# Moving the expert-weight casts from GpSimd to ScalarE, with other PSUM banks for the attention and an earlier output store

## The chip, the cores and the metric

The kernel runs on one Trainium2 chip, on all 8 of its NeuronCores. Each core computes one batch element (2048 tokens of width 1024) and holds the whole set of weights to itself; nothing passes between the cores. The metric is the device time in microseconds (us) of the slowest core.

## What is computed

Two transformer layers, with a layer norm ahead of each. The layer's input, its attention and its feed-forward part are added up:

```python
xn = layernorm(x)
x = x + L0_attn(xn, Wq, bq, Wk, bk) + L0_moe(xn, Wr, W1, W2)
xn = layernorm(x)
x = x + L1_attn(xn, Wq, Wk, Wv, Wo) + L1_ffn(xn, weight, alpha, bias)
```

- L0_attn: 16 heads of 64, no mask; the values are the keys (v = k).
- L0_moe: 8 experts, W1 [8, 1024, 4096] and W2 [8, 4096, 1024]. All 8 experts are computed for every token, `relu(h @ W1) @ W2`, and the two with the largest router values are summed with weights.
- L1_attn: 16 query heads, 4 key/value heads, rotary embedding, causal.
- L1_ffn: one matrix of 1024 x 1024 whose entries are set to -1, 0 or 1.

## The kernel before

The activations stay in SBUF, features on the partitions: `xT` (float32) and its normed copy `xnT` (bf16), each as 8 chunks of 128 features by 2048 tokens. Tokens are worked in 4 tiles of 512 (`NTAU`, `NT`). Each engine has one queue that is filled in the order in which the Python code emits instructions; a small class `PB` adds the semaphore waits from keys that an instruction reads and writes (`pb.op(engine, ...)`, `pb.dma(queue, ...)`). No scheduler reorders anything: an instruction that waits holds up everything that was emitted behind it on its engine.

The stages, in the order of emission: layer norm 0; attention 0; the mixture of experts; layer norm 1; attention 1; the ternary feed-forward part with the output projection of attention 1 woven in; the store.

**Attention.** `attn_stream_gen` works through tiles of 512 queries for a pair of heads. For each block of 128 keys (`kc`) TensorE writes two score blocks into banks 0 and 1, or 2 and 3 for odd `kc` (L339); ScalarE takes the exponential of both in one instruction (L362); TensorE then multiplies the previous block's exponentials with the values (L352) and accumulates 65 rows for each of the two heads in a bank of its own. Here these are banks 4 and 5 (`bankB` in the profile) for even tiles, and 6 and 7 (`bank`) for odd tiles. The finish of a tile (the reciprocal of the row sums: L444, L447 on ScalarE, L450, L452 on VectorE, L454, L458 on TensorE, L462, L469, L473 on VectorE; in layer 1 L1058 to L1078) is emitted in the next tile, at its `kc == 1`, ahead of that tile's first L352. In attention 0 the projections of the next pair of heads (L495, L502, L516, L523, moved out of PSUM by ScalarE in L506, L527, L530) are woven in: one such chunk, then three steps of the stream. They use banks 2 and 3. There are 8 pairs of heads with 4 tiles each in either layer.

**Experts.** The weights come as float32. For each of the 8 experts 16 pieces of W1 (128x2048) and 32 pieces of W2 (128x1024) are loaded into one of two slots of `stg`, cast to bf16 into the single buffer `castb` (L701, L718) and stored to DRAM (`sw1`, `sw2`). The loads, the casts and the stores all stand in GpSimd's queue, in the order load, cast, store, load, and so on, 384 times; each store also waits for the store before it. GpSimd has nothing else to do, so this queue runs from the time that the slots of `stg` are free of attention 0's own weights, beside attention 0 and the expert computation. All 384 steps are emitted ahead of the expert computation. That one runs over experts and token tiles: for each group of four blocks SyncE's queue loads 1 MB of bf16 W1 into `w1buf`, TensorE does 8 matmuls for each of 32 blocks (L749) into banks 0 to 3 in turn, and ScalarE applies relu (L757) from the bank into `hid`; then 8 x 32 matmuls with W2 (L770), scaled and added by VectorE (L778, L782). Ahead of it stands the router: 16 short chains in which ScalarE has one instruction each (L665).

**Store.** The last eight instructions of GpSimd's queue store the eight chunks of `xT`, 1 MB each. `xch(dc)` is final once both of that chunk's updates (L1239, L1136) for the four token tiles are done; the loop finishes one chunk after the other.

Of the kernel before, what the change touches and what calls it, by code (L numbers as in the profile page):

```python
# [12 lines left out]
AX = mybir.AxisListType  # L13
# [137 lines left out]
def build_nc(stages=ALL_STAGES, dbg=None):  # L151
# [27 lines left out]
    out_t = out_d.rearrange("(c p) t -> c p t", p=128)  # L179

    with ExitStack() as ctx:
# [139 lines left out]
        def attn_stream_gen(tiles):  # L321
# [8 lines left out]
            for ti, t in enumerate(tiles):  # L330
                nkc = t["nkc"]
                av0 = 4 + 2 * (ti % 2)
                for kc in range(nkc + 1):
# [11 lines left out]
                    if kc >= 1:  # L345
                        kp = kc - 1
                        qp = 2 * (kp % 2)
                        for h12 in range(2):
                            q4 = qp + h12
                            avb = av0 + h12  # L350
                            pb.op("tensor",
                                  lambda e, kp=kp, h12=h12, q4=q4, avb=avb, t=t, nkc=nkc: e.matmul(  # L352
                                      bank[avb][0:65, :], t["vap"](kp, h12),
                                      t["expb"][:, q4 * NT:(q4 + 1) * NT],
                                      start=(kp == 0), stop=(kp == nkc - 1)),
                                  reads=[f"e{q4}", t["vkeys"][h12]],
                                  writes=([f"b{avb}"] if kp == nkc - 1 else []),
                                  wait=(pb._dep_waits((), [f"b{avb}"]) if kp == 0 else []))
# [20 lines left out]
                for h12 in range(2):  # L379
                    pending_fin[h12] = (lambda t=t, h12=h12, avb=av0 + h12:  # L380
                                        t["fins"][h12](avb))
# [6 lines left out]
        def emit_attn0(xn_done):  # L388
# [49 lines left out]
            def mk_fin(h12, tgt_fn):  # L438
                def fin(avb):
# [40 lines left out]
            def prologue_chunks(hp):  # L480
# [29 lines left out]
                for mt in range(16):  # L510
                    def ktm(mt=mt, hp=hp, par=par, vA=vA, vB=vB):
                        bnk = bank[2 + (mt % 2)]
                        bkkey = f"b{2 + (mt % 2)}"
# [21 lines left out]
                def norms(hp=hp, par=par, qT=qT, kT=kT):  # L535
                    for (src, skey, coli) in ((qT, f"qT{par}", 0), (kT, f"kT{par}", 4)):
                        pb.op("vector", lambda e, src=src: e.tensor_tensor(
                            expb[:, :], src[:], src[:], ALU.mult),
                            reads=[skey], writes=["e0", "e1", "e2", "e3"])
                        for tau in range(NTAU):  # L540
                            pb.op("tensor", lambda e, tau=tau: e.matmul(
                                bank[2][0:1, :], onescol[:, :],
                                expb[:, tau * NT:(tau + 1) * NT], start=True, stop=True),
                                reads=[f"e{tau}", "onescol"], writes=["b2"])
                            pb.op("vector", lambda e, tau=tau, coli=coli: e.reduce_max(
                                CP[0:1, coli + tau:coli + tau + 1], bank[2][0:1, :], AX.X),
                                reads=["b2"], writes=[f"cp{coli + tau}"])
# [17 lines left out]
                        bank[2][:, 0:1], onesf[:, :], CP[0:1, 11:12],  # L565
                        start=True, stop=True),
                        reads=["cpn", "onesf"], writes=["b2"])
                    pb.op("vector", lambda e, par=par: e.tensor_copy(
                        CP[:, 12 + par:13 + par], bank[2][:, 0:1]),
                        reads=["b2"], writes=[f"neg{par}"])  # L570
# [38 lines left out]
        def emit_moe0(xn_done):  # L609
# [80 lines left out]
            for ex in range(NEXP):  # L690
                for fg in range(8):
                    for half in range(2):
# [8 lines left out]
                        pb.op("gpsimd", lambda e, slot=slot: e.tensor_copy(  # L701
# [6 lines left out]
                for dc in range(8):  # L708
                    for qt in range(4):
# [8 lines left out]
                        pb.op("gpsimd", lambda e, slot=slot: e.tensor_copy(  # L718
# [70 lines left out]
        def emit_attn1(xn_done):  # L789
# [150 lines left out]
            for kvc in range(2):  # L940
                for tau in range(NTAU):
                    t0 = tau * NT
                    pj = 2 + tau % 2
# [10 lines left out]
                for mt in range(16):  # L954
                    bnk = bank[2 + mt % 2]
                    bkkey = f"b{2 + mt % 2}"
# [16 lines left out]
            for kvc in range(2):  # L973
# [4 lines left out]
                for tau in range(NTAU):  # L978
                    pb.op("tensor", lambda e, tau=tau: e.matmul(
                        bank[2][0:1, :], onescol[:, :],  # L980
                        expb[:, tau * NT:(tau + 1) * NT], start=True, stop=True),
                        reads=[f"e{tau}", "onescol"], writes=["b2"])
                    pb.op("vector", lambda e, tau=tau: e.reduce_max(
                        CP[0:1, tau:tau + 1], bank[2][0:1, :], AX.X),
                        reads=["b2"], writes=[f"cp{tau}"])
# [13 lines left out]
            for hp in range(DCH):  # L999
# [6 lines left out]
                for tau in range(NTAU):  # L1006
                    t0 = tau * NT
                    pj = 2 + tau % 2
# [12 lines left out]
                for tau in range(NTAU):  # L1021
                    pb.op("tensor", lambda e, tau=tau: e.matmul(
                        bank[2][0:1, :], onescol[:, :],
                        expb[:, tau * NT:(tau + 1) * NT], start=True, stop=True),
                        reads=[f"e{tau}", "onescol"], writes=["b2"])
                    pb.op("vector", lambda e, tau=tau: e.reduce_max(
                        CP[0:1, tau:tau + 1], bank[2][0:1, :], AX.X),
                        reads=["b2"], writes=[f"cp{tau}"])
# [17 lines left out]
                    bank[2][:, 0:1], onesf[:, :], CP[0:1, 11:12],  # L1046
                    start=True, stop=True),
                    reads=["cpn", "onesf"], writes=["b2"])
                pb.op("vector", lambda e: e.tensor_copy(CP[:, 13:14], bank[2][:, 0:1]),
                      reads=["b2"], writes=["neg1"])  # L1050

                def mk_fin1(h12, ytgt, ybase, t0):
                    def fin(avb):
                        bb = h12
# [227 lines left out]
        if dbg == "xn0":  # L1282
            for dc in range(DCH):
# [74 lines left out]
```

How the kernel before makes its waits and increments, by code:

```python
            def body(eng):  # L131
                for w, fn, incs in ops:
                    for s, c in w:
                        eng.wait_ge(sems[s], c)
                    ins = fn(eng)
                    for s, n in incs:
                        ins.then_inc(sems[s], n)
```

## Time and profile before

| | us |
|---|---|
| median of 2 runs (7091.28 and 7559.44) | 7325.36 |
| profiled execution | 7085.0 |
| span of its slowest core (core 1) | 7083.5 |
| spans of the 8 cores | 7025.6 to 7083.5 |
| TensorE busy / ScalarE / VectorE / GpSimd | 5404.0 / 1929.0 / 1441.1 / 1063.1 |
| mean granted TensorE clock, as a share of full speed | 0.874 to 0.878 |

The span goes from the first to the last instruction of a core. Busy times of TensorE (PE) are modelled at their ends, so a stretch is best read by the start times of its instructions. All rows below are of core 1.

### The profile page before, as it was taken

The numbers are of one execution on the slowest core, as the hardware profiler recorded it, in microseconds if no ns is written. First come the engines' busy times: TensorE is split into PE (matmuls) and PEld (weight loads), VectorE is DVE, ScalarE is ACT, GpSimd is POOL, SyncE is SP. The second block draws the span as 40 slices with busy tenths as digits, with TensorE's granted clock in tenths as the row PEclk, the third lists the DMA queues.
The fourth block names the chain that finished last, engine by engine and source line by source line (L and its number), as shares of the span: only waits on it lengthen the run. The fifth ranks groups of instructions, "written<-read, shape, count | busy, mean of one in ns | idle before, by whom it ended". The sixth has DMA issues, their size and how long they took to land.

```text
span 7083.5 us, 83359 instructions; the slowest of 8 cores (7025.6 to 7083.5 us)
## 1 busy us (share of the span) xinstructions
PE 5404.0 (76%) x23303; PEld 2151.8 (30%) x23303; DVE 1441.1 (20%) x2660; ACT 1929.0 (27%) x2813; POOL 1063.1 (15%) x1169
## 2 busy tenths in 40 slices
PE   3566666664899989999889999999999635555536
PEld 0222222211344334334334444444444111111112
DVE  5211212123010101001010101010110443333335
ACT  0354454552111111111111121211112024554530
POOL 0233333333222222222222100000000000000000
PEclk9887787776999999999999999999999656666768
DMA  2434444344777777777777543444444100000012
GB/s 65 162 109 135 125 128 136 116 145 140 240 237 227 231 235 219 232 233 218 224 231 214 187 154 143 149 149 149 149 151 158 36 12 12 4 6 4 4 48 72
DMA packets 205108, 989.73 MB, mean 140 GB/s; under 512 B 23014, under 2 KB 33518, under 8 KB 137082
## 3 DMA queue, kind: packets, MB, share of 16 engines
q1 hardware_dynamic: 92922, 573.29, 23.9%
q0 software_dynamic: 111744, 411.09, 19.5%
q8 instruction: 210, 3.44, 0.2%
q14 instruction: 232, 1.90, 0.1%
HBM read 841.69 MB, written 142.61 MB: 139 GB/s over the span
## 4 chain that ended last, share of the span: by engine, by line
PE 59%; DMA 13%; ACT 12%; DVE 10%; issue 6%; DVEq 0%; ACTq 0%; SPq 0%; POOL 0%; POOLq 0%
PE bankA L749 21%; PE bankA L770 21%; ACT exp L362 7%; DMA w1buf<-sw 5%; DMA w2buf<-sw 5%; PE bankA L339 3%; PE bankB L352 2%; PE bank L352 2%; PE bankA L495 2%; ACT rtmpB L921 1%; PE bankA L1125 1%; PE bankA L1226 1%; PE bankA L516 1%; DVE rhl L452 1%; DVE xnTs L292 1%
## 5 line engine op out<-in xcount | busy, mean ns | idle before, releaser
L770 PE MATMUL bankA<-hid,w2buf 128*128 128x512 bf16 x8192 | 1797.0, 381 | 107.6 <-DMA w2buf<-sw 78.5
L749 PE MATMUL bankA<-xnTs,w1buf 128*128 128x512 bf16 x8192 | 1808.3, 383 | 79.9 <-DMA w1buf<-sw 79.7
L757 ACT ACTIVATE hid<-bankA 128x512 bf16<-128x512 f32 x1024 | 611.5, 597 | 3160.7 <-PE bankA L749 3160.7
L770 PEld LDWEIGHTS bankA<-hid,w2buf 128*128 128x128 bf16 x8192 | 798.3, 98 | 1106.3 <-issue 171.7
L749 PEld LDWEIGHTS bankA<-xnTs,w1buf 128*128 128x128 bf16 x8192 | 801.1, 99 | 1096.4 <-issue 167.5
L362 ACT ACTIVATE exp<-bankA,colpool 128x1024 bf16<-128x1024 f32 x832 | 908.8, 1113 | 486.8 <-PE bankA L339 454.5
L778 DVE TENSOR_TENSOR mtmp<-bankA,cbs 128x512 f32<-128x512 f32 x256 | 177.0, 692 | 3414.9 <-PE bankA L770 3414.9
L718 POOL CAST castb<-stg 128x1024 bf16<-128x1024 f32 x256 | 271.0, 1059 | 1458.0 <-DMA stg<-l0w 1458.0
L701 POOL CAST castb<-stg 128x2048 bf16<-128x2048 f32 x128 | 246.2, 1924 | 1032.7 <-DMA stg<-l0w 1032.7
L110 POOL DMA_DIRECT2D stg<-l0w x384 | 332.2, 865 | 219.9 <-DVE wkbf L310 201.8
L817 POOL IOTA invfr<- 1x128 f32 x1 | 0.2, 241 | 1703.6 <-ACT c L821 1703.6
L110 POOL DMA_DIRECT2D sw<-castb x384 | 210.2, 547 | 211.1 <-POOL castb L718 140.7
L450 DVE CAST rhl<-rrow 1x512 bf16<-1x512 f32 x64 | 39.0, 609 | 963.6 <-ACT rrow L447 963.6
L110 POOL DMA_DIRECT2D outT<-xTs x8 | 4.2, 536 | 1340.5 <-DVE xTs L1136 1340.5
L782 DVE TENSOR_TENSOR xTs<-xTs,mtmp 128x512 f32<-128x512 f32 x256 | 186.2, 727 | 27.3 <-DVE mtmp L778 0.9
L352 PE MATMUL bank<-exp,vG 128*65 128x512 bf16 x384 | 144.1, 442 | 56.5 <-DVE exp L373 36.6
L454 PE MATMUL bankA<-rhl,onesb 1*128 1x512 bf16 x64 | 34.2, 535 | 182.6 <-DVE rhl L450 182.6
L373 DVE TENSOR_TENSOR exp<-exp,cmaskS 128x512 bf16<-128x512 bf16 x256 | 97.4, 422 | 303.1 <-ACT exp L362 303.1
L339 PE MATMUL bankA<-qT,kT 64*128 64x512 bf16 x640 | 154.4, 466 | 0.1
L1068 PE MATMUL bankA<-rhl,onesb 1*128 1x512 bf16 x64 | 36.7, 574 | 153.1 <-DVE rhl L1064 153.1
L352 PE MATMUL bankB<-exp,vG 128*65 128x512 bf16 x256 | 108.2, 500 | 44.4 <-DVE exp L373 35.1
L339 PE MATMUL bankA<-qT0a,kT0a 64*128 64x512 bf16 x512 | 114.3, 411 | 25.3 <-ACT vB0b L530 13.6
(232 smaller groups left out, 3395.8 us busy)
## 6 DMA issues: line engine op xcount, KB each, us to landing
w1buf<-sw SPq DMA_DIRECT2D x256, 1024.0 KB, 6.9
w2buf<-sw SPq DMA_DIRECT2D x256, 1024.0 KB, 6.8
stg<-l0w POOLq DMA_DIRECT2D x128, 1024.0 KB, 7.4
stg<-l0w POOLq DMA_DIRECT2D x256, 512.0 KB, 5.6
sw<-castb POOLq DMA_DIRECT2D x128, 512.0 KB, 3.3
sw<-castb POOLq DMA_DIRECT2D x256, 256.0 KB, 3.3
xTs<-xT SPq DMA_DIRECT2D x8, 1024.0 KB, 16.6
wtf<-l1wt SPq DMA_DIRECT2D x16, 512.0 KB
```

What stands on the lines that cost most here:

```text
L110: self.on(qeng, lambda e, o=out, i=in_: e.dma_start(o, i), wait=w, inc=[(sem, 16)])
L339: lambda e, kc=kc, h12=h12, q4=q4, t=t: e.matmul(bank[q4][:, :], t["klhsT"](kc, h12), t["qrhs"][h12], start=True, stop=True),
L352: lambda e, kp=kp, h12=h12, q4=q4, avb=avb, t=t, nkc=nkc: e.matmul(bank[avb][0:65, :], t["vap"](kp, h12), t["expb"][:, q4 * NT:(q4 + 1) * NT],
L362: lambda e, pp=pp, t=t: e.activation(t["expb"][:, pp * NT:(pp + 2) * NT], bankA[:, pp * NT:(pp + 2) * NT], AF.Exp, bias=t["negcol"]),
L495: e.matmul(bnk[:, :], wbf[:, dc * 1024 + hp * 128: dc * 1024 + (hp + 1) * 128], xnch(dc)[:, t0:t0 + NT], start=(dc == 0), stop=False),
L701: pb.op("gpsimd", lambda e, slot=slot: e.tensor_copy(castb[:, 0:2048], stg[:, slot * 2048:(slot + 1) * 2048]), reads=[f"stg{slot}"], write ...
L718: pb.op("gpsimd", lambda e, slot=slot: e.tensor_copy(castb[:, 0:1024], stg[:, slot * 2048:slot * 2048 + 1024]), reads=[f"stg{slot}"], writ ...
L749: e.matmul(bnk[:, :], w1buf[:, slot * 4096 + dc * NT + fp * 128: slot * 4096 + dc * NT + (fp + 1) * 128], xnch(dc)[:, t0:t0 + NT], start=( ...
L757: pb.op("scalar", lambda e, f=f, bnk=bnk: e.activation(hid[:, f * NT:(f + 1) * NT], bnk[:, :], AF.Relu), reads=[bkkey], writes=[f"hid{f % ...
L770: e.matmul(bnk[:, :], w2buf[:, slot * 4096 + fc * 128:slot * 4096 + (fc + 1) * 128], hid[:, fc * NT:(fc + 1) * NT], start=(fc == 0), stop= ...
L778: pb.op("vector", lambda e, bnk=bnk, mslot=mslot: e.tensor_tensor(mtmp[:, mslot * NT:(mslot + 1) * NT], bnk[:, :], cbs[:], ALU.mult), read ...
L782: pb.op("vector", lambda e, dc=dc, t0=t0, mslot=mslot: e.tensor_tensor(xch(dc)[:, t0:t0 + NT], xch(dc)[:, t0:t0 + NT], mtmp[:, mslot * NT: ...
```

## The change

Five edits. The casts of the expert weights go from GpSimd to ScalarE; their loads and stores stay in GpSimd's queue. The attention's value products always use banks 4 and 5. The projections use banks 6 and 7 in place of 2 and 3 (in `norms` bank 7, in layer 1's norms bank 4). The finish in layer 1 broadcasts through banks 6 and 7 in place of 0 and 1 (in layer 0 it keeps 0 and 1). The output stores wait for their own chunk only.

```diff
@@ attn_stream_gen
-                av0 = 4 + 2 * (ti % 2)
...
-                            avb = av0 + h12
...
-                                      bank[avb][0:65, :], t["vap"](kp, h12),
+                                      bank[4 + h12][0:65, :], t["vap"](kp, h12),
...
-                                  wait=(pb._dep_waits((), [f"b{avb}"]) if kp == 0 else []))
+                                  wait=(pb._dep_waits((), [f"b{4 + h12}"]) if kp == 0 else []))
@@ prologue_chunks, proj and ktm (the same in layer 1's projections)
-                            bnk = bank[2 + tau % 2]
-                            bkkey = f"b{2 + tau % 2}"
+                            bnk = bank[6 + tau % 2]
+                            bkkey = f"b{6 + tau % 2}"
@@ emit_moe0, pieces of W1
-                        pb.op("gpsimd", lambda e, slot=slot: e.tensor_copy(
+                        pb.op("scalar", lambda e, slot=slot: e.copy(
                             castb[:, 0:2048],
                             stg[:, slot * 2048:(slot + 1) * 2048]),
                             reads=[f"stg{slot}"], writes=["castb0"])
@@ emit_moe0, pieces of W2
-                        pb.op("gpsimd", lambda e, slot=slot: e.tensor_copy(
+                        pb.op("scalar", lambda e, slot=slot: e.copy(
                             castb[:, 0:1024],
                             stg[:, slot * 2048:slot * 2048 + 1024]),
@@ mk_fin1
-                        bb = h12
+                        avb = 4 + h12
+                        bb = 6 + h12
@@ the end
-        final_waits = [("dv", pb.cnt["dv"]), ("sc", pb.cnt["sc"]),
-                       ("pe", pb.cnt["pe"]), ("gp", pb.cnt["gp"])]
         for dc in range(DCH):
-            pb.dma("gpsimd", out_t[dc], xch(dc), "dst",
-                   reads=[f"x{dc}"], wait=final_waits)
+            pb.dma("gpsimd", out_t[dc], xch(dc), "dst", reads=[f"x{dc}"])
```

ScalarE's queue around the start of the experts, before: the last finish of attention 0, the router's sixteen instructions, then the 1024 relus.

```order
L447 ACTIVATE rrow<-rrow 1x512
L665 ACTIVATE colpool<-colpool 128x1 x16
L757 ACTIVATE hid<-bankA 128x512 x1024
L259 COPY rows_ln<-bankB 1x512
L261 COPY rows_ln<-bank 1x512
```

The same place in the changed kernel, where L699 and L716 are the casts, L755 the relu and L663 the router; the dots stand for six more pairs of the two casts.

```order
L445 ACTIVATE rrow<-rrow 1x512
L663 ACTIVATE colpool<-colpool 128x1 x16
L699 CAST castb<-stg 128x2048 x16
L716 CAST castb<-stg 128x1024 x32
...
L699 CAST castb<-stg 128x2048 x16
L716 CAST castb<-stg 128x1024 x32
L755 ACTIVATE hid<-bankA 128x512 x1024
L259 COPY rows_ln<-bankB 1x512
```

All 384 casts now stand on ScalarE behind attention 0 and the router, and ahead of the first relu.

GpSimd's queue at the start of the weight steps, before, with the semaphores that each waits for (pga, pgb: the loads; ppw: the stores; gp: GpSimd's own instructions).

```order
L110 DMA stg<-l0w1 128x4x512 [waits stga,dv]
L701 CAST castb<-stg 128x2048 [waits pga]
L110 DMA sw1<-castb 128x2048 [waits gp]
L110 DMA stg<-l0w1 128x4x512 [waits stgb,dv]
L701 CAST castb<-stg 128x2048 [waits pgb,ppw]
```

The same place in the changed kernel (sc: ScalarE's instructions).

```order
L110 DMA stg<-l0w1 128x4x512 [waits stga,dv]
L110 DMA sw1<-castb 128x2048 [waits sc]
L110 DMA stg<-l0w1 128x4x512 [waits stgb,dv]
L110 DMA sw1<-castb 128x2048 [waits ppw,sc]
L110 DMA stg<-l0w1 128x4x512 [waits pga]
```

The first load still goes out early; the first store waits for ScalarE's first cast, and the second load stands behind that store.

TensorE's queue at a change of tile in attention 0, before: the finish's four small matmuls, then the new tile's first value products.

```order
L339 MATMUL bankA<-qT0a,kT0a 128x512 x2
L454 MATMUL bankA<-rhl0,onesb 128x512
L458 MATMUL bankA<-rhl0,onesb 128x512
L454 MATMUL bankA<-rhl0,onesb 128x512
L458 MATMUL bankA<-rhl0,onesb 128x512
L352 MATMUL bank6<-exp0,vA0a 65x512
L352 MATMUL bank7<-exp0,vB0a 65x512
```

The same place in the changed kernel (L350 is the value product).

```order
L338 MATMUL bankA<-qT0a,kT0a 128x512 x2
L452 MATMUL bankA<-rhl0,onesb 128x512
L456 MATMUL bankA<-rhl0,onesb 128x512
L452 MATMUL bankA<-rhl0,onesb 128x512
L456 MATMUL bankA<-rhl0,onesb 128x512
L350 MATMUL bankB<-exp0,vA0a 65x512
L350 MATMUL bankB<-exp0,vB0a 65x512
```

The order is the same; the value products now write the banks (4 and 5, `bankB`) that the previous tile's finish still has to read.

## Rows read from the trace of the kernel before

**Rows 1.** The view by stretches; columns: stretch, length, busy us (instructions) of each engine, clock, DMA share, GB/s.
```profile
1000.00:1500.00 500.00, 318.02 (x1389) 103.75 (x1387) 105.12 (x153) 248.91 (x346) 167.63 (x178) 0.79 0.43 137
1640.00:1726.00 86.00, 11.20 (x147) 7.60 (x148) 41.86 (x209) 3.24 (x16) 26.27 (x32) 0.50 0.41 122
1800.00:4000.00 2200.00, 2031.68 (x9083) 888.86 (x9081) 217.62 (x304) 334.42 (x560) 528.36 (x578) 0.98 0.75 228
4020.00:5549.00 1529.00, 1515.25 (x6967) 680.39 (x6964) 161.42 (x235) 250.78 (x420) 0.00 (x0) 1.00 0.40 148
```

**Rows 2.** The groups by line, whole span; busy us, mean ns, idle before and releaser.
```profile
L757 ACT ACTIVATE hid<-bankA 128x512 bf16<-128x512 f32 x1024 | 611.5, 597 | 3160.7 <-PE bankA L749 3160.7
L1202 ACT ACTIVATE wsgn<-wtf 128x1024 bf16<-128x1024 f32 x8 | 8.5, 1057 | 78.9 <-DMA wtf<-l1wt 68.1 <-DVE wtb L1214 10.9
```

**Rows 3.** GpSimd's timeline beside attention 0: start us, us, what, idle before.
```profile
228.75 1.89 POOL L701 CAST castb<-stg 128x2048 bf16<-128x2048 f32 x1 [6.15 <-DMA stg<-l0w]
231.19 0.53 POOL L110 DMA_DIRECT2D sw<-castb  x1 [0.54 <-POOL castb L701]
231.72 0.77 POOL L110 DMA_DIRECT2D stg<-l0w  x1
238.45 1.89 POOL L701 CAST castb<-stg 128x2048 bf16<-128x2048 f32 x1 [5.97 <-DMA stg<-l0w]
...
901.63 1.04 POOL L718 CAST castb<-stg 128x1024 bf16<-128x1024 f32 x1 [3.92 <-DMA stg<-l0w]
...
908.67 1.04 POOL L718 CAST castb<-stg 128x1024 bf16<-128x1024 f32 x1 [3.99 <-DMA stg<-l0w]
```

**Rows 4.** GpSimd's timeline: the first cast of experts 0 to 3.
```profile
208.36 2.06 POOL L701 CAST castb<-stg 128x2048 bf16<-128x2048 f32 x1 [4.96 <-DMA stg<-l0w]
...
611.12 1.89 POOL L701 CAST castb<-stg 128x2048 bf16<-128x2048 f32 x1 [5.45 <-DMA stg<-l0w]
...
1005.73 1.89 POOL L701 CAST castb<-stg 128x2048 bf16<-128x2048 f32 x1 [5.48 <-DMA stg<-l0w]
...
1394.15 1.89 POOL L701 CAST castb<-stg 128x2048 bf16<-128x2048 f32 x1 [5.60 <-DMA stg<-l0w]
```

**Rows 5.** The timeline where the experts begin, ScalarE and TensorE.
```profile
1721.38 0.20 ACT L665 ACTIVATE colpool<-colpool 128x1 f32<-128x1 f32 x1 [4.81 <-DVE colpool L662]
1729.89 0.60 ACT L757 ACTIVATE hid<-bankA 128x512 bf16<-128x512 f32 x1 [8.31 <-PE bankA L749]
...
1725.98 5.18 PE L749 MATMUL bankA<-xnTs,w1buf 128*128 128x512 bf16 x15
```

**Rows 6.** The chain that ended last, pieces of the experts: start us, us, what.
```profile
4027.00 55.41 PE bankA L770 x256
...
5493.87 55.43 PE bankA L770 x256
...
5539.79 9.51 PE bankA L770 x44
```

**Rows 7.** The end of the span: the last VectorE instruction, the stores, the time to landing.
```profile
7057.10 0.69 DVE L1136 TENSOR_TENSOR xTs<-xTs,wtmp 128x512 f32<-128x512 f32 x1
7058.55 4.22 POOL L110 DMA_DIRECT2D outT<-xTs  x8 [1340.51 <-DVE xTs L1136]
...
DMA to landing us min/median/max: 4.4/11.7/18.6
```

**Rows 8.** The timeline at a change of tile in attention 0.
```profile
841.49 0.63 PE L352 MATMUL bank<-exp,vB0b 128*65 128x512 bf16 x1
842.03 0.69 DVE L469 TENSOR_TENSOR t1s<-bankB,rb 64x512 f32<-64x512 f32 x1
```

**Rows 9.** The groups by line within 240 to 1631 us (attention 0); idle before and releaser.
```profile
L339 PE MATMUL bankA<-qT0b,kT0b 64*128 64x512 bf16 x512 | 115.2, 423 | 18.7 <-ACT vB0a L530 10.2 <-ACT kT0a L506 4.1 <-ACT qT0a L506 4.1
L339 PE MATMUL bankA<-qT0a,kT0a 64*128 64x512 bf16 x512 | 114.3, 411 | 25.3 <-ACT vB0b L530 13.6 <-ACT qT0b L506 5.8 <-ACT kT0b L506 5.5
L516 PE MATMUL bankA<-wkbf,xnTs 128*128 128x128 bf16 x896 | 78.1, 237 | 31.7 <-ACT exp L362 31.7
```

More of the change, by code:

```diff
@@ L356, in attn_stream_gen @@
                                   reads=[f"e{q4}", t["vkeys"][h12]],
-                                  writes=([f"b{avb}"] if kp == nkc - 1 else []),
-                                  wait=(pb._dep_waits((), [f"b{avb}"]) if kp == 0 else []))
+                                  writes=([f"b{4 + h12}"] if kp == nkc - 1 else []),
+                                  wait=(pb._dep_waits((), [f"b{4 + h12}"]) if kp == 0 else []))
                     if kc < nkc:
@@ L511, in ktm @@
                     def ktm(mt=mt, hp=hp, par=par, vA=vA, vB=vB):
-                        bnk = bank[2 + (mt % 2)]
-                        bkkey = f"b{2 + (mt % 2)}"
+                        bnk = bank[6 + (mt % 2)]
+                        bkkey = f"b{6 + (mt % 2)}"
                         for dc in range(DCH):
@@ L564, in norms @@
                     pb.op("tensor", lambda e: e.matmul(
-                        bank[2][:, 0:1], onesf[:, :], CP[0:1, 11:12],
+                        bank[7][:, 0:1], onesf[:, :], CP[0:1, 11:12],
                         start=True, stop=True),
-                        reads=["cpn", "onesf"], writes=["b2"])
+                        reads=["cpn", "onesf"], writes=["b7"])
                     pb.op("vector", lambda e, par=par: e.tensor_copy(
-                        CP[:, 12 + par:13 + par], bank[2][:, 0:1]),
-                        reads=["b2"], writes=[f"neg{par}"])
+                        CP[:, 12 + par:13 + par], bank[7][:, 0:1]),
+                        reads=["b7"], writes=[f"neg{par}"])
                 ch.append(norms)
@@ L954, in emit_attn1 @@
                 for mt in range(16):
-                    bnk = bank[2 + mt % 2]
-                    bkkey = f"b{2 + mt % 2}"
+                    bnk = bank[6 + mt % 2]
+                    bkkey = f"b{6 + mt % 2}"
                     for dc in range(DCH):
@@ L979, in emit_attn1 @@
                     pb.op("tensor", lambda e, tau=tau: e.matmul(
-                        bank[2][0:1, :], onescol[:, :],
+                        bank[4][0:1, :], onescol[:, :],
                         expb[:, tau * NT:(tau + 1) * NT], start=True, stop=True),
-                        reads=[f"e{tau}", "onescol"], writes=["b2"])
+                        reads=[f"e{tau}", "onescol"], writes=["b4"])
                     pb.op("vector", lambda e, tau=tau: e.reduce_max(
-                        CP[0:1, tau:tau + 1], bank[2][0:1, :], AX.X),
-                        reads=["b2"], writes=[f"cp{tau}"])
+                        CP[0:1, tau:tau + 1], bank[4][0:1, :], AX.X),
+                        reads=["b4"], writes=[f"cp{tau}"])
                 pb.op("vector", lambda e, kvc=kvc: e.reduce_max(
@@ L1022, in emit_attn1 @@
                     pb.op("tensor", lambda e, tau=tau: e.matmul(
[L1023 removed]
+                        bank[4][0:1, :], onescol[:, :],
                         expb[:, tau * NT:(tau + 1) * NT], start=True, stop=True),
[L1025 removed]
+                        reads=[f"e{tau}", "onescol"], writes=["b4"])
                     pb.op("vector", lambda e, tau=tau: e.reduce_max(
[L1027 to L1028 removed]
+                        CP[0:1, tau:tau + 1], bank[4][0:1, :], AX.X),
+                        reads=["b4"], writes=[f"cp{tau}"])
                 pb.op("vector", lambda e: e.reduce_max(CP[0:1, 8:9], CP[0:1, 0:4], AX.X),
@@ L1045, in emit_attn1, with fin @@
                 pb.op("tensor", lambda e: e.matmul(
-                    bank[2][:, 0:1], onesf[:, :], CP[0:1, 11:12],
+                    bank[4][:, 0:1], onesf[:, :], CP[0:1, 11:12],
                     start=True, stop=True),
-                    reads=["cpn", "onesf"], writes=["b2"])
-                pb.op("vector", lambda e: e.tensor_copy(CP[:, 13:14], bank[2][:, 0:1]),
-                      reads=["b2"], writes=["neg1"])
+                    reads=["cpn", "onesf"], writes=["b4"])
+                pb.op("vector", lambda e: e.tensor_copy(CP[:, 13:14], bank[4][:, 0:1]),
+                      reads=["b4"], writes=["neg1"])
                 def mk_fin1(h12, ytgt, ybase, t0):
-                    def fin(avb):
-                        bb = h12
+                    def fin():
+                        avb = 4 + h12
+                        bb = 6 + h12
                         hi = rhl1[0:1, (2 * h12) * NT:(2 * h12 + 1) * NT]
```

19 lines of the change are left out of this document (9 added, 10 removed).

## The prediction

> **What bounds the kernel now.** I read the view by stretches first [rows 1], since the shares of the whole span mix four regimes. From 4020 to 5549 us TensorE is busy for 1515 of 1529 us at a granted clock of 1.00 (2.4 GHz): the experts are pure TensorE time there, and GpSimd does nothing. From 1800 to 4000 us TensorE is busy for 2032 of 2200 us, with DMA at 0.75 and GpSimd in 578 instructions: the weight steps run beside the experts and cost them something, but do not set the pace. From 1000 to 1500 us (attention 0) GpSimd is as active, 178 instructions, while ScalarE is busy for half of the time. So the conversion of 384 weight pieces is hidden: beside attention 0, beside the router, and beside the first half of the experts. The groups by line say what ScalarE does in the expert stage [rows 2]: it waits 3161 us for the matmuls of L749 and works 611 us. It looks like an engine with room to spare. The question is where in its queue the new work stands.
>
> The two listings of ScalarE's queue under the change answer it. In the changed kernel all 384 casts stand behind attention 0 and the router and ahead of the first of 1024 relus. ScalarE can't begin a cast before attention 0 is over, and can't give a relu before the last cast is done. TensorE has four banks for L749; after four blocks of 8 matmuls it must wait for a relu. GpSimd's listing shows the other half: the second load stands behind the first store, which waits for ScalarE's first cast, so only one piece is loaded ahead. The weight conversion ceases to be hidden anywhere and becomes a stage of its own between router and experts.
>
> **The casts: length of the new stage.** Its step is the old one, load, cast, store issue, next load, in strict turn. In the timeline of GpSimd a piece of W1 takes 9.70 us from cast to cast (228.75 to 238.45): 1.89 us of cast, 0.54 us until the store is issued, 0.53 us for that, and 6.73 us from the issue of the load to the next cast; a piece of W2 takes 7.04 us (901.63 to 908.67) [rows 3]. For a whole expert, 16 + 32 pieces, I take differences of first casts while only attention runs beside [rows 4]: 402.8, 394.6 and 388.4 us. I take the last, since the new stage runs beside idle engines; 16 x 9.70 + 32 x 7.04 = 380.5 is the low bound and 402.8 the high one. Eight experts less the last changeover (8.6 us of step, of which 1.0 is cast: 7.6): 8 x 388.4 - 7.6 = 3099.6 us; bounds 3036 and 3215.
>
> ScalarE in place of GpSimd changes a step a little. The cast itself: ScalarE writes 128x1024 from SBUF float32 to bf16 in 1057 ns (L1202), GpSimd in 1040 ns [rows 2, 3], which is nothing. The handoff: cast to store is 0.54 us within GpSimd; from VectorE to GpSimd's output store it was 0.76 us (7057.79 to 7058.55) [rows 7]. No row shows ScalarE releasing such a store. From a gap of zero (-0.54 a step, -207 us) to 0.76 with as much again for the way from the load to another engine (+0.44, +169 us), I take +0.1 us a step, between the same-engine and the cross-engine row: 384 x 0.1 = +38 us.
>
> Start: the router's last ScalarE instruction is at 1721.38 [rows 5]; the first piece has long landed, so the casts begin at 1721.7. Last cast ends at 1721.7 + 3099.6 + 38 = 4859.3. The first relu came at 1729.9 [rows 5]; it moves by 3129.4 us. TensorE by then has the first four blocks ready, three of which it had not at the old first relu: 3 x 1.73 (55.41 us for 256 matmuls [rows 6]) = 5.2 us back. **Term 1: +3124 us.**
>
> **The experts alone.** With the conversion finished ahead, no weight transfer competes with the loads of `w1buf` and `w2buf`. Before, the stage took 1725.98 to 5549.30 (5539.79 + 9.51) = 3823.3 us [rows 5, 6]. Undisturbed, thirteen rounds of one expert and one token tile took 4027.00 to 5493.87, 112.84 us each [rows 6]; 32 rounds take 3610.8. **Term 2: -212.5 us.** Zero is the bound on one side (if the clock or the loads are no better), -212.5 the other.
>
> On that clock a page speaks against me. In the stretch of 4020 to 5549 us the granted clock is 1.00 [rows 1], with all eight cores at work. The Trainium skill's page "TensorE: Matmul & The Clock Gate", section "Seeing it yourself", warns that dense matmuls on most cores of a die bring the whole die to 13/16 of the clock while they last. By that rule 3610.8 us would be an estimated 4444 us; by the row it is 3610.8. The trace does not agree with the page in this stretch, so I keep the row, and give the other case as a rival.
>
> **The output stores.** They no longer wait for the end of everything: chunk 0's store goes out seven eighths of the last stage earlier, and only the last chunk stands after the last VectorE instruction. Before, 7058.55 to 7083.5 = 24.9 us followed; now one transfer follows, 4.4 to 11.7 us by its landing times, of which the least loaded is nearest: 6 us [rows 7]. The matmuls beside don't use DMA there. **Term 3: -19 us** (-13 to -20.5).
>
> **Banks 4 and 5 for every tile.** At a change of tile the second head's first value product started at 841.49, while the finish of the other pair of banks was still to read its own in L469 until 842.03 + 0.69 = 842.72 [rows 8]. Now it waits for that read; with some 0.14 us for the release, it starts at 842.86, 1.37 us later. The first head's read was over earlier and costs nothing. Behind the waiting product TensorE has the next scores and ScalarE the next exponential, so it is on the path. It happens in 3 of 4 tiles (the last tile's finish is flushed before the next pair starts), 8 pairs, 2 layers: 48 x 1.37. **Term 4: +66 us** (0 if the wait is covered, 66 otherwise).
>
> **Banks 6 and 7 for the projections.** TensorE waited 31.7 us in L516 for an exponential to free banks 2 or 3, and 18.7 + 25.3 us in L339 for ScalarE to move a projection out of them [rows 9]: 75.7 us, all gone. ScalarE is the next to be late, with 249 of 500 us busy [rows 1] not by much; I take -60 of it. **Term 5: -60 us** (-76 to 0). The finish of layer 1 through banks 6 and 7, and GpSimd's absence as a neighbour of VectorE, I put at nothing: the scores that write bank 0 next stand behind those value products in TensorE's queue anyway.
>
> **Sum**, against the profiled execution: 7083.5 + 3124 - 212.5 - 19 + 66 - 60 = 9982, plus the 1.5 us that its time lies above the span: 9984, say **9980 us**. That execution (7085.0) stands near the faster of the two runs shown (7091), 240 us under their median of 7325; the two runs lie 468 us apart, so a median of few runs of the changed kernel may lie that much above.
>
> **Rivals.** (a) *The clock.* The dense stretch grows from 1.5 ms to 3.6 ms with no gap for DMA, and the chip grants less. For it: attention 0 shows 0.79 and the far spacing of the two runs; against it: 1.00 for 1.5 ms on end [rows 1]. At 0.79 the stage takes 3610.8 / 0.79 = 4571, +960: 10940 us. The page's 13/16 would give an estimated 10815. (b) *Slow steps.* The steps take what they took beside the experts: 578 GpSimd instructions in 2200 us against 178 in 500 [rows 1] is a rate lower by 1.355, so 388.4 becomes 526 an expert and the total 11080. Against it: nothing else moves data in the new stage. (c) *Loads run ahead.* The two slots let the next load overlap cast and store: 16 x 6.7 + 32 x 4.9 (7.04 less 1.04, 0.54 and 0.53) = 264 an expert, 995 us less: 8985. Against it: the load stands behind the store in GpSimd's queue. (d) *Not slower.* The relus get past the casts, because ScalarE does not keep its emitted order or because the conversion still begins at 208 us; then the experts start at 1726 as before, and with terms 3 to 5 the time is 7072. It decides from the point where the stage costs less than 226 us, 0.6 us a step; a single cast of W2 takes 1.04. The listings exclude it unless the change does not do what it says.
>
> **How the numbers follow.** My forecast 0.86; (a) 0.06, (b) 0.03, (c) 0.03, (d) 0.01, and 0.01 for something else on the faster side. The forecast's own range comes from the bounds of stage length (-64, +115), handoff (-245, +131), term 2 (up to +212), and the rest; these ends don't come together, and some 9770 to 10230 holds it. To keep 8 in 10 with a spread of runs like that shown, I reach up to 10450. About 2% is what a measurement of this kernel can tell from no change; slower by over 2% are forecast, (a), (b), (c) and part of the rest: 0.98; within 2% 0.01; faster 0.01.
>
> **What would show it.** In the changed profile: GpSimd issues one load near 203 us and then nothing until about 1722; from there to about 4860 us TensorE is idle at a low clock, ScalarE shows 384 casts busy for about a sixth of the time, and waits for the loads, DMA at about 0.4; the relus start after the last cast; 32 rounds of 112.8 us follow at clock 1.00; the stores begin within the last stage, 6 us follow its last VectorE instruction. Wrong would be a first cast before 1600 us, relus between casts, an expert's pieces under 370 or over 410 us, a round over 114 us, or attention 0 changed by over 60 us.

## The result and the profile after

| | before | changed | prediction |
|---|---|---|---|
| median of all runs, us | 7093.7 (10 runs) | 10081.1 (11 runs) | 9980 |
| profiled execution, us | 7085.0 | 9868.8 | 9984 |
| ratio | 1 | 1.396 [1.391, 1.401] | 1.409 |

The change makes the kernel slower by 40%. In some executions the cores of one die ran at a lower clock; the interval of the ratio leaves these out and the median of 10081 holds them, so the terms are read from the profiled execution, and in the experiments from cores that were not held back, each against the same core of the other kernels.

The page's slices of the changed kernel, 247 us each (rows: busy tenths of an engine, the granted clock, the DMA share):

```profile
PE   3666661000000000000899999999999998355555
ACT  0555552111111111111111111111111111155551
POOL 0000000111111111111000000000000000000000
PEclk9878775555555555555999999999999998577777
DMA  2000002344343443443344434444444343000002
```

From slice 8 to slice 19 TensorE does next to nothing (33 instructions in the second row below) and its clock stands at 0.5 (1.2 GHz). GpSimd's work, which used to run beside attention 0 and the first half of the experts, lies in exactly those slices. The view by stretches says the same in microseconds:

```profile
240.00:1500.00 1260.00, 827.82 (x3720) 272.79 (x3717) 257.34 (x426) 682.49 (x924) 0.00 (x0) 0.78 0.00 1
1610.00:4700.00 3090.00, 9.35 (x33) 3.38 (x32) 0.69 (x1) 504.51 (x379) 529.66 (x759) 0.50 0.41 130
4730.00:8327.00 3597.00, 3567.69 (x16400) 1602.08 (x16398) 371.35 (x541) 608.48 (x1019) 0.00 (x0) 1.00 0.41 149
```

From 1610 to 4700 us ScalarE is busy for 505 of 3090 us and DMA for 0.41: no engine is busy for most of the stage. That looks like a chain of latencies; the run with loads ahead tests it. The groups by line name the waits (busy, mean ns, idle before and what ended it):

```profile
L747 PE MATMUL bankA<-xnTs,w1buf 128*128 128x512 bf16 x8192 | 1778.8, 380 | 3105.3 <-ACT hid L755 2712.5
L716 ACT CAST castb<-stg 128x1024 bf16<-128x1024 f32 x256 | 267.6, 1045 | 1579.4 <-DMA stg<-l0w 1579.4
L699 ACT CAST castb<-stg 128x2048 bf16<-128x2048 f32 x128 | 243.0, 1898 | 1026.9 <-DMA stg<-l0w 1026.9
```

The old L749 never waited for a relu. TensorE now waits once, for 2712.5 us, for the first relu. The other 392.8 us of its idle time end with weight loads, nearly all of it with the first one: L747 starts at 2003 us, once expert 0 is converted, fills its four banks and stops. ScalarE waits 2606 us for loads between its casts. The two ends of the stage in ScalarE's timeline, the last router instruction and first cast, the last cast and first relus:

```profile
1606.17 0.20 ACT L663 ACTIVATE colpool<-colpool 128x1 f32<-128x1 f32 x1 [4.09 <-DVE colpool L660]
1606.28 1.88 ACT L699 CAST castb<-stg 128x2048 bf16<-128x2048 f32 x1
...
4722.12 1.04 ACT L716 CAST castb<-stg 128x1024 bf16<-128x1024 f32 x1 [5.98 <-DMA stg<-l0w]
4723.19 2.07 ACT L755 ACTIVATE hid<-bankA 128x512 bf16<-128x512 f32 x4
```

GpSimd's timeline from its start, which answers to [rows 3, 4]: one load, then nothing for 1405 us.

```profile
202.44 0.91 POOL L110 DMA_DIRECT2D stg<-l0w  x1 [201.74 <-DVE wkbf L310]
1608.73 0.54 POOL L110 DMA_DIRECT2D sw<-castb  x1 [1405.39 <-ACT castb L699]
1609.33 0.77 POOL L110 DMA_DIRECT2D stg<-l0w  x1
```

The store goes out at 1608.73, 0.57 us after the cast's end at 1608.16, much the gap that GpSimd had behind its own cast (0.54 us). Later in the stage it is 0.54 us here too: a cast at 2403.00 lasts 1.90 us, and its store goes out at 2405.44. The chain of the expert stage, against [rows 6], has no DMA piece left:

```profile
4776.27 55.41 PE bankA L768 x256
...
8159.39 55.41 PE bankA L768 x256
...
8272.11 28.00 PE bankA L768 x129
```

Thirty rounds in 3383.1 us are 112.77 each. The end, against [rows 7]:

```profile
9859.00 0.69 DVE L1135 TENSOR_TENSOR xTs<-xTs,wtmp 128x512 f32<-128x512 f32 x1
9860.24 0.53 POOL L110 DMA_DIRECT2D outT<-xTs  x1 [13.28 <-DVE xTs L1135]
...
DMA to landing us min/median/max: 4.2/4.2/5.2
```

Stage by stage, from the first and last starts of each line (before on core 1, after on core 5, the slowest of each):

| stage | before | after | difference |
|---|---|---|---|
| start to the router's last ScalarE instruction | 1721.4 | 1606.2 | -115.2 |
| from there to the first relu | 8.5 | 3117.0 | +3108.5 |
| first relu to the last matmul of the experts | 3819.0 | 3603.9 | -215.1 |
| layer norm 1 and the rest up to attention 1 | 313.9 | 314.7 | +0.8 |
| attention 1, first projection to last exponential | 973.8 | 999.5 | +25.7 |
| up to and through the last feed-forward part | 220.5 | 217.7 | -2.8 |
| after the last VectorE instruction's start | 26.4 | 8.0 | -18.4 |
| sum | 7083.5 | 9867.0 | +2783.5 |

One row was not foreseen: the start up to the router is 115 us shorter, where 27 were forecast. The experiments go to that, and to the question whether the engine of the casts or their place makes the loss.

### The profile page after: what moved, and what is told of

The parts are those of the page before. It is cut to its first block, busy times and chain, and to the rows that moved or that the text cites. A ratio compares the mean times of both kernels' runs of the same rounds, so it can differ in the third digit from the quotient of the medians.

```text
span 9867.0 us, 84588 instructions; the slowest of 8 cores (9852.4 to 9867.0 us)
## 1 busy us (share of the span) xinstructions
PE 5307.5 (54%) x23303; PEld 2146.6 (22%) x23303; DVE 1402.8 (14%) x2660; ACT 2434.4 (25%) x3197; POOL 543.6 (6%) x785
## 4 chain that ended last, share of the span: by engine, by line
PE 47%; DMA 23%; ACT 13%; DVE 7%; issue 7%; POOL 2%; ACTq 0%; DVEq 0%; POOLq 0%; SPq 0%
DMA stg<-l0w 21%; PE bankA L768 18%; PE bankA L747 18%; ACT exp L360 5%; PE bankB L350 3%; ACT castb L716 3%; ACT castb L699 2%; POOL sw L110 2%; PE bankA L338 2%; PE bank L493 1%; ACT rtmpB L919 1%; PE bankA L1124 1%; PE bankA L1225 1%; DVE rb L1075 0%; DVE rb L460 0%
## 5 line engine op out<-in xcount | busy, mean ns | idle before, releaser
L747 PE MATMUL bankA<-xnTs,w1buf 128*128 128x512 bf16 x8192 | 1778.8, 380 | 3105.3 <-ACT hid L755 2712.5
L768 PE MATMUL bankA<-hid,w2buf 128*128 128x512 bf16 x8192 | 1773.4, 379 | 28.7 <-ACT hid L755 28.6
L747 PEld LDWEIGHTS bankA<-xnTs,w1buf 128*128 128x128 bf16 x8192 | 799.4, 98 | 4094.0 <-issue 3140.1
L755 ACT ACTIVATE hid<-bankA 128x512 bf16<-128x512 f32 x1024 | 611.1, 597 | 2937.7 <-PE bankA L747 2937.6
L716 ACT CAST castb<-stg 128x1024 bf16<-128x1024 f32 x256 | 267.6, 1045 | 1579.4 <-DMA stg<-l0w 1579.4
L699 ACT CAST castb<-stg 128x2048 bf16<-128x2048 f32 x128 | 243.0, 1898 | 1026.9 <-DMA stg<-l0w 1026.9
L350 PE MATMUL bankB<-exp,vG 128*65 128x512 bf16 x640 | 258.5, 467 | 132.4 <-DVE exp L371 75.4
L448 DVE CAST rhl<-rrow 1x512 bf16<-1x512 f32 x64 | 26.3, 411 | 879.9 <-ACT rrow L445 879.9
L350 PE MATMUL bankB<-exp,vA0b 128*65 128x512 bf16 x256 | 109.5, 428 | 60.2 <-ACT exp L360 53.6
L350 PE MATMUL bankB<-exp,vA0a 128*65 128x512 bf16 x256 | 109.2, 426 | 58.7 <-ACT exp L360 53.3
L452 PE MATMUL bankA<-rhl,onesb 1*128 1x512 bf16 x64 | 35.3, 551 | 177.1 <-DVE rhl L448 177.1
L350 PEld LDWEIGHTS bankB<-exp,vG 128*65 128x65 bf16 x640 | 61.3, 119 | 282.0 <-issue 281.9
L1067 PE MATMUL bank<-rhl,onesb 1*128 1x512 bf16 x64 | 35.8, 559 | 152.2 <-DVE rhl L1063 152.2
```

What stands on the lines that cost most here:

```text
L350: lambda e, kp=kp, h12=h12, q4=q4, t=t, nkc=nkc: e.matmul(bank[4 + h12][0:65, :], t["vap"](kp, h12), t["expb"][:, q4 * NT:(q4 + 1) * NT], ...
L699: pb.op("scalar", lambda e, slot=slot: e.copy(castb[:, 0:2048], stg[:, slot * 2048:(slot + 1) * 2048]), reads=[f"stg{slot}"], writes=["cas ...
L716: pb.op("scalar", lambda e, slot=slot: e.copy(castb[:, 0:1024], stg[:, slot * 2048:slot * 2048 + 1024]), reads=[f"stg{slot}"], writes=["ca ...
L747: e.matmul(bnk[:, :], w1buf[:, slot * 4096 + dc * NT + fp * 128: slot * 4096 + dc * NT + (fp + 1) * 128], xnch(dc)[:, t0:t0 + NT], start=( ...
L755: pb.op("scalar", lambda e, f=f, bnk=bnk: e.activation(hid[:, f * NT:(f + 1) * NT], bnk[:, :], AF.Relu), reads=[bkkey], writes=[f"hid{f % ...
L768: e.matmul(bnk[:, :], w2buf[:, slot * 4096 + fc * 128:slot * 4096 + (fc + 1) * 128], hid[:, fc * NT:(fc + 1) * NT], start=(fc == 0), stop= ...
```

## The experiments

**Only the casts.** The kernel before, with the two casts on ScalarE.

```diff
-                        pb.op("gpsimd", lambda e, slot=slot: e.tensor_copy(
+                        pb.op("scalar", lambda e, slot=slot: e.copy(
```

> The kernel before with only the casts moved to ScalarE. Theory that the place in the queue is the whole loss: 384 casts stand between router and first relu, the stage between them lasts 3117 us as in the changed kernel, the experts take 3604 us after it, total about 9960 us (9940 to 9980). Under theory P of the projection banks the router ends at 1705 to 1721 us; under theory G (GpSimd's absence) near 1620 to 1640 us, total about 9880.

Measured: 10052.7 us once; cores 4 to 7 spanned 9926.8 to 9939.2. ScalarE's timeline on core 5:

```profile
1691.16 0.20 ACT L665 ACTIVATE colpool<-colpool 128x1 f32<-128x1 f32 x1 [4.10 <-DVE colpool L662]
1691.27 1.88 ACT L701 CAST castb<-stg 128x2048 bf16<-128x2048 f32 x1
...
4793.63 2.07 ACT L757 ACTIVATE hid<-bankA 128x512 bf16<-128x512 f32 x4
```

The stage between router and relu lasts 3102 us, and the experts 3602 after it. The casts alone bring the whole loss. The router's end, 1691.2 on core 5, lies between the two forecasts for it: before it was at 1726.2 on this core. So up to there the absence of GpSimd's casts gives 35 us on core 5, and on cores 4, 6 and 7 it gives 23, 24 and 11.

**Only the casts' place.** The casts stay on ScalarE, 48 of them ahead of the first relu, the rest woven into the experts. One step (load, cast, store) is emitted at each of 12 places a round:

```diff
+            for _ in range(48):
+                one_step()
...
+                        if fg % 2 == 1:
+                            one_step()
...
+                        one_step()
```

> The changed kernel with the casts still on ScalarE, but only expert 0's 48 stand ahead of the first relu; the other 336 are woven into the expert computation, 12 in each round of one expert and one token tile (one after every second group of W1, one after each block of W2). If the place in the queue makes the loss: the first relu comes near 1606 + 391 = 2000 us, the expert stage takes 3604 to 4250 us (a conversion beside the experts took some 540 us an expert before, a round set of four takes 451), total 7150 to 7800 us. If ScalarE as the engine of the casts makes it (384 steps that cost the same wherever they stand): near 9870 us.

Measured: 7941.3 us, beside 7067.6 for the kernel before. The first relu came at 2004.7 us on core 6, 407 after the router's end at 1597.4; the experts took 4393 us, more than the 4250 I allowed. The same 384 casts on the same engine cost 874 us here against 2784, so 1900 us of the loss belong to the place. Of the 874, some 400 are the 48 casts that still stand ahead of the first relu. What is left shows at `castb` and at the relu:

```profile
L710 ACT CAST castb<-stg x384: 1036/1045/1900, 1597.5 to 5935.9; 128x1024 bf16<-128x1024 f32 x128, 128x2048 bf16<-128x2048 f32 x64
...
  DMA stg<-l0w: 2306.3, 292
  ACT hid L760: 632.0, 48
```

ScalarE waits 2306 us in 292 casts for their loads, and while it waits no relu passes; in turn the stores waited 632 us that are put down to a relu in front of the cast. The expert stage took 789 us more than the 3604 of the changed kernel. Of these TensorE waited 432 us for relus (22 times): a queue that waits, in small pieces. It waited another 256 us for weight loads; the remaining 100 were not taken apart.

**Loads ahead.** The changed kernel, with load n+1 emitted before cast and store of piece n.

```diff
+            steps[0][0]()
+            for n, (load, finish) in enumerate(steps):
+                if n + 1 < len(steps):
+                    steps[n + 1][0]()
+                finish()
```

> The changed kernel with each load issued ahead of the previous piece's cast and store. The stage between router and first relu lasted 3117 us. If it is a chain of latencies (load, cast, store issue in strict turn), overlapping the load with the rest leaves 6.7 us a piece of W1 and 4.9 us a piece of W2, 264 us an expert: the stage takes about 2110 to 2400 us, total 8860 to 9150 us. If the stage is bound by what the transfers can move (about 130 GB/s were seen), it stays at 3000 to 3117 us and the total near 9800 to 9870.

Measured: 8827.2 us, once, a little under the forecast; the stage lasts from 1599.3 to 3619.7 on core 6, 2020 us, 253 an expert. A piece of W2 takes 4.6 us where it took 7.2 (ScalarE's timeline, core 6):

```profile
1702.54 1.04 ACT L710 CAST castb<-stg 128x1024 bf16<-128x1024 f32 x1 [3.87 <-DMA sw<-castb]
1707.43 1.04 ACT L710 CAST castb<-stg 128x1024 bf16<-128x1024 f32 x1 [3.85 <-DMA sw<-castb]
1711.78 1.04 ACT L710 CAST castb<-stg 128x1024 bf16<-128x1024 f32 x1 [3.30 <-DMA sw<-castb]
```

The stage was a chain of latencies, not bound by what transfers can move: they moved 200 GB/s here (1610 to 3600 us) against 130. The wait ahead of a cast is no longer the load but the previous store, which still reads the single `castb`.

**Casts back on GpSimd.** The changed kernel without the cast edit; the rest of the change alone.

> The changed kernel with the casts returned to GpSimd; banks and stores stay as changed. It tells what the rest of the change is worth. In the changed kernel the router ended at 1606 us and not at 1721. Theory P: that gain comes from the projections' own banks, so the router ends near 1610 to 1625 here too; the total is 7085 less some 100 (attention 0) less 18 (stores) plus 26 (value banks in attention 1) plus 10 (a longer overlap of conversion and experts): about 7000 us, 1 to 1.5% faster than before. Theory G: the gain came from GpSimd's absence as VectorE's neighbour; then the router ends near 1690 to 1700 and the total is near 7075 us.

> The same kernel as in the run with the casts returned to GpSimd, on another chip and with more rounds, to settle its ratio to the kernel before. Its undisturbed cores spanned 6943 to 6984 us there, against 7035 to 7053 us before. By the terms measured (attention 0 -127 from the projections' banks, +29 and +27 from the value banks in the two attentions, stores -19) it should take 0.986 to 0.990 of the kernel before, about 6990 to 7010 us. The rival: the experts start 100 us earlier with fewer weights ready and give it back; then the ratio is over 0.995.

Cores 4 to 7 of the first run spanned 6943.2 to 6984.1 us, against 7031.4 to 7052.8 before. The second gave the ratio: 0.989 [0.985, 0.993], with a profiled span of 7004.5. The rest of the change is a gain of 1.1%, and the rival (the earlier start of the experts given back) does not hold. On core 5 of the first run the router ends at 1617.2, on cores 4, 6 and 7 at 1626 to 1635: some us later than theory P has it, and far from theory G's 1690.

**Only the value banks.** The kernel before with one number changed.

```diff
-                av0 = 4 + 2 * (ti % 2)
+                av0 = 4
```

> The kernel before with the value products always in banks 4 and 5, and nothing else changed. It measures the term that the prediction put at 1.37 us in each of 48 changes of tile. Expected by the prediction: attention 0 and attention 1 each longer by 33 us, total +66 us (0.9%). The rival: the wait hides behind ScalarE's exponential or VectorE's work and the total moves by less than 20 us. After the profile of the changed kernel (attention 1 longer by 26 us) I expect +50 to +66.

Measured: no ratio came out of this run, but cores 4 to 7 spanned 7092.0 to 7141.9 us against 7031.4 to 7052.8, +67 for the medians. The wait is there (who waited for whom, core 5, the two attentions apart):

```profile
PE bankB L352 <- DVE t1s L469: 28.3, 24, 1.5
...
PE bankB L352 <- DVE yT L1078: 28.0, 24, 1.2
```

Exactly 24 times in each, 1.18 us a time. The changed kernel's timeline shows one of them, against [rows 8]:

```profile
702.43 0.68 DVE L467 TENSOR_TENSOR t1s<-bankB,rb 64x512 f32<-64x512 f32 x1
...
703.26 0.61 PE L350 MATMUL bankB<-exp,vB0a 128*65 128x512 bf16 x1 [1.17 <-DVE t1s L467]
```

The five kernels side by side give attention 0 in parts. Each row is the last update of attention 0 (duration min/median/max in ns, first and last start), all on core 5: before; value banks only; casts back; casts only; the full change.

```profile
L473 DVE TENSOR_TENSOR xTs<-xTs,t1s x64: 683/689/2384, 306.2 to 1641.9; 64x512 f32<-64x512 f32 x64
L473 DVE TENSOR_TENSOR xTs<-xTs,t1s x64: 683/689/2125, 300.5 to 1661.8; 64x512 f32<-64x512 f32 x64
L471 DVE TENSOR_TENSOR xTs<-xTs,t1s x64: 683/689/1579, 298.5 to 1529.4; 64x512 f32<-64x512 f32 x64
L473 DVE TENSOR_TENSOR xTs<-xTs,t1s x64: 683/686/690, 298.4 to 1615.9; 64x512 f32<-64x512 f32 x64
L471 DVE TENSOR_TENSOR xTs<-xTs,t1s x64: 683/686/690, 302.0 to 1530.8; 64x512 f32<-64x512 f32 x64
```

From the first projection to that update, differences on cores 4, 5, 6 and 7: value banks +28, +20, +37, +55 us, mean +35; the projections' banks (casts back less value banks) -117, -132, -127, -135, mean -128; the casts' absence (casts only less before) -14, -24, -14, -3, mean -13. Each is one trace against one trace, and the kernel before spreads over 16 us on these cores, so the small two are known to some 10 us. In the rows the maximum falls from 2384 to 690 ns once GpSimd does no casts.

**Loads ahead, casts on GpSimd.** Both ideas that gained, together; then with the W2 pieces in the two halves of `castb` in turn.

> Casts on GpSimd, banks and stores as changed, and each load issued ahead of the previous piece's cast and store, so that it overlaps them. If a step is then load alone (6.7 and 4.9 us), an expert's conversion takes about 264 to 300 us beside attention 0 instead of 393, five experts are ready when the router ends and the rest costs the expert stage less: total 30 to 80 us under the run with the casts back, about 6930 to 6970 us. The rival: the extra transfers in flight only slow each other down and the loads of the experts, and the total stays within 20 us of the run with the casts back, or rises.

> The same kernel as in the run with casts on GpSimd and loads ahead. Its clock was low in that run's profile, so that its expert stage could not be read. Conversion ends near 2580 us instead of 3970. If that relieves the experts, the total is 30 to 80 us under the run with the casts back. If denser transfers beside attention 0 and the experts' start only cost elsewhere (attention 0 was 22 to 77 us longer there), the two are equal within 20 us.

> The version with casts on GpSimd and loads ahead, with the W2 pieces using the two halves of castb in turn, so that a cast no longer waits for the store just before it (that wait took 1180 us over 383 casts). If that wait sets the pace, a W2 step falls from 4.6 to about 4 us and conversion ends some 100 to 200 us earlier; the expert stage gains 0 to 20 us: total 0.980 to 0.985 of the kernel before. If the transfers set it, conversion ends where it did (2610 to 2690 us) and the total stays at 0.983.

```diff
+                c0 = 0 if i < 16 else slot * 1024
+                cb = castb[:, c0:c0 + wd]
+                keys = ["castb0", "castb1"] if i < 16 else [f"castb{slot}"]
```

The first run is inconclusive: its profile had a granted clock of 0.81 in the expert stage (2600 to 3900 us) and its four times run from 7064 to 7631. The second spans 6956.4 us on its slowest core against 7004.5 for the casts back, 48 less; by the lowest times, 6958.1 against 6984.0, it is 26 less. The forecast was 30 to 80, so the gain is at its lower end; no interval came out. Conversion ended between 2609 and 2692 us in place of 3867 to 3994, and the expert stage took 3706 to 3749 us (core 5: 3737, against 3778). Attention 0 changed by -10 to +20 us from core to core, +7 in the mean. GpSimd's casts there waited for the stores alone (core 4):

```profile
L710 POOL CAST castb<-stg x384: 1040/1042/2667, 208.3 to 2682.4; 128x1024 bf16<-128x1024 f32 x128, 128x2048 bf16<-128x2048 f32 x64
...
  DMA sw<-castb: 1180.4, 383
```

With the halves in turn the ratio to the kernel before is 0.978 [0.975, 0.981], a little better than the forecast of 0.980 to 0.985, and the lowest time 6924.4 us. In its profile, which had granted clocks of 0.81 to 0.82, conversion ends between 2337 and 2448 us, earlier than forecast, and on core 4 the casts' wait for the store falls from 1180 to 485 us: that wait did set the pace. That is the best version found; it beats both kernels.

## Why the prediction was right, and where a term was off

**The mechanism and the main term.** Right, with its numbers. The place of the casts in ScalarE's queue made the loss: the casts by themselves reproduce it, and with the same casts placed elsewhere two thirds of it are gone. From the router's last ScalarE instruction to the first relu it took 3117 us against a predicted 3138. Inside, two small errors cancel in part: an expert's 48 pieces took 391 us (388.4 forecast, 17 too low over eight), and the 0.1 us a step for the handoff to another engine, 38 us, does not exist: the gap is 0.54 to 0.57 us across engines and 0.54 within GpSimd [rows 3]. My other row, 0.76 from VectorE to the output store [rows 7], was the wrong one to lean on. That store waited for four engines; in the changed kernel the last store waits for its own chunk alone and goes out 0.55 us after VectorE's last instruction (9859.69 to 9860.24). That the four waits made the difference was not tested.

**The experts alone** (term 2): -212.5 forecast; from first relu to last matmul it is -215.1, of which I had booked 5.2 with term 1. Rounds of 112.77 against 112.84. The mean granted clock over these 3597 us was 1.00 (2.4 GHz) on core 5, and it was 1.00 on the other seven cores too. Rival (a) does not hold for this execution. It was a live one all the same: the casts-only kernel was granted 0.97 to 0.98 in this stage on cores 0 to 3, and the first run with casts on GpSimd and loads ahead 0.81 to 0.83 on all eight cores from 2600 to 3900 us. What decides between these clocks no run shows. The page "TensorE: Matmul & The Clock Gate" of the Trainium skill, section "Seeing it yourself", gives 13/16 for dense matmuls on three or more cores of a die. The changed kernel's trace does not agree with it; the 0.81 of that other run does.

**The stores** (term 3): -19 forecast, -18.4.

**The value banks** (term 4): 1.37 us in 48 places, +66 forecast. The place and the count were right; the price is 1.18 us (28.3 / 24), which makes 57 us of wait; the two attentions together grew by 67. In attention 1 the stage grew by 32 us on core 5 with the value banks alone (972.4 to 1004.1), and by 27 in the full change (999.5). So the full change's other edits, of which the finish and the projections through other banks touch attention 1, gave some 5 back; I had put the finish at nothing, and the two were not taken apart.

**The projections' banks** (term 5): this step failed in size, and beyond its bounds. "75.7 us, all gone. [...] I take -60 of it. Term 5: -60 us (-76 to 0)"; measured is -128 in attention 0 alone. It also set off one of my own signs of being wrong, attention 0 changed by over 60 us: it became 101 to 112 us shorter on cores 4 to 7. The sum of TensorE's waits at two lines was taken as the most that could be won. What the starts of successive key projections show is the length of the cycle instead, one chunk and three steps of the stream. Before:

```profile
711.12 0.61 PE L516 MATMUL bankA<-wkbf,xnTs 128*128 128x128 bf16 x8 [0.78 <-ACT exp L362]
715.26 0.61 PE L516 MATMUL bankA<-wkbf,xnTs 128*128 128x128 bf16 x8
720.75 0.61 PE L516 MATMUL bankA<-wkbf,xnTs 128*128 128x128 bf16 x8 [0.78 <-ACT exp L362]
```

and in the changed kernel:

```profile
710.44 0.61 PE L514 MATMUL bank<-wkbf,xnTs 128*128 128x128 bf16 x8
714.42 0.61 PE L514 MATMUL bank<-wkbf,xnTs 128*128 128x128 bf16 x8
718.41 0.61 PE L514 MATMUL bank<-wkbf,xnTs 128*128 128x128 bf16 x8
```

Two cycles took 9.63 us and take 7.97: 0.83 us a chunk, where the waits of two cycles at L516 and L339, 0.78 and 0.25, come to 0.5 a chunk. With the casts back on GpSimd and the banks as changed (second run, core 5) it is the same, 7.98 us, so the banks do it and not GpSimd's absence:

```profile
710.67 0.61 PE L514 MATMUL bank<-wkbf,xnTs 128*128 128x128 bf16 x8
714.66 0.61 PE L514 MATMUL bank<-wkbf,xnTs 128*128 128x128 bf16 x8
718.65 0.61 PE L514 MATMUL bank<-wkbf,xnTs 128*128 128x128 bf16 x8
```

A pair of engines that hand banks to each other waits on both sides: TensorE for ScalarE to free bank 2, ScalarE for the late scores and projections. The waits of attention 0 on core 5, value banks alone against casts back, show both. TensorE's waits for ScalarE at L516, L339 and L495, 88 us, are gone, while those at the value product grew by 11. ScalarE's waits for scores fell from 245 to 191 us and those for projections from 154 to 113. The prediction counted the first side only, and there it left out L495. No sum of one engine's waits gives the 132 us that were won on this core.

**GpSimd's absence** as a neighbour, put at nothing: -13 us in attention 0 in the mean of cores 4 to 7. Up to the router's end it is -23 in the mean and -35 on core 5, of which attention 0 has 24 and the router chain 6 (65 us in place of 71). The casts of L448 take 411 ns on average where L450 took 609, the length that they have in attention 1. This is what VectorE showed with and without GpSimd casting beside it; what the two engines share, these runs do not say.

**The sum** was 115 us above the profiled execution, 1.2%: terms 4 and 5 give 95 of it with the GpSimd share, terms 1 and 2 together 18, the rest 2. The median of 10081 lies 212 us above the profiled execution. That the stated 9980 came within 1% of it is in part luck: the terms were too high by 115, and the 9980 left that spread out.

**Rivals.** (a) the clock: above. (b) slow steps: no, 391 us an expert. (c) loads ahead: not in this order; made so, the stage is 2020 us (2112 by the rival's own working). (d) not slower: no relu passes a cast. One more sign of being wrong, a first cast before 1600 us, was set too near: on core 5 it came at 1606.3, but the router ended as early as 1594.7 on other cores, since attention 0 was shorter.

## What to carry to other kernels

An engine that is idle for three quarters of the time is not free for work whose place in its queue is fixed: ask what stands ahead of the new instruction, what stands behind it, and who waits for that. Work that is hidden because it has a queue of its own loses its cover when one step of it moves to a shared queue, even if the step takes the same microsecond there. Between two engines that hand buffers to each other, read the gain of a further buffer from the length of the whole cycle, not from the sum of one engine's waits; and if a chain of load, convert, store is hidden but long, issue the next load ahead of the conversion.

## What the runs showed of the hardware

- A cast of 128x2048 from float32 to bf16 in SBUF took 1.898 us at the median on ScalarE and 1.893 on GpSimd; 128x1024 took 1.045 and 1.040.
- A semaphore from ScalarE to a waiting DMA issue of GpSimd cost hardly more than one from GpSimd itself: 0.54 to 0.57 us against 0.54.
- VectorE's cast of 1x512 elements (L450, L448) took up to 2104 ns beside GpSimd's casts (core 5) and at most 416 ns without them, with the median unchanged at 411 to 415.
- Dense matmuls on all eight cores were granted a clock of 1.00 (2.4 GHz) for 3.6 ms in the changed kernel's profiled execution, and of 0.81 to 0.83 for 1.3 ms in that of another kernel.
